# Reordering the work around the first token pair of a fused conditional-residual kernel: block chains ahead of combination splits, b1s cleared at another place, three copies on another engine

## The reference, cut to what matters

```
x = x + W0[a]^T x                                  # mixes the 64 tokens of a sequence, W0[a] is 64x64
x = x + x W1 + (x A1[a]) B1[a]                     # rank 16
x = x + x W2^T + 0.5 (x A2[l]) B2^T                # rank 32
x = x + x W3^T + 2 sum_e gate_e(x) (x A3_e^T) B3_e # 8 experts of rank 16, the top 2 of the logits
                                                   # x Wr^T + 5 onehot(g), softmax over the 2
```

## Time and profile before

| | |
|---|---|
| median of 3 runs | 541.6 us (541.12 to 542.69) |
| the profiled execution | 540.56 us, of it 538.8 us from first to last instruction |
| granted TensorE clock, mean | 0.997 |
| TensorE busy | 526.5 us |
| VectorE, ScalarE, GpSimd busy | 300.3, 183.4, 163.3 us |
| first token pair on TensorE | from 250.2 to 297.9 us |

### The profile page before, as it was taken

The page is one execution under the profiler, slowest core; times in us unless marked ns, Lnnn a source line. Parts: engine busy times, 40 slices in busy tenths (PEclk is TensorE's granted clock), DMA queues, the critical chain, the costliest instruction groups (busy, mean ns, idle before and its releaser), DMA issues.

```text
span 538.8 us, 8930 instructions
## 1 busy us (share of the span) xinstructions
PE 526.5 (98%) x2764; PEld 459.4 (85%) x2764; DVE 300.3 (56%) x638; ACT 183.4 (34%) x339; POOL 163.3 (30%) x250
## 2 busy tenths in 40 slices
PE   8999999999999999999889999999999999999996
PEld 7999999998888888888667888888888888888885
DVE  3851323389723323379868674664747547466463
ACT  5641312135122323255153333233323333233322
POOL 2501000002111111128643335444354343542400
PEclk9999999999999999999899999999999999999999
DMA  8803020013440202040430422214223142132302
GB/s 280 301 29 132 2 78 16 1 54 123 142 151 3 79 0 79 1 157 6 141 94 22 129 82 89 86 77 126 83 70 94 74 132 88 56 95 78 126 21 78
DMA packets 23246, 46.79 MB, mean 87 GB/s; under 512 B 6820, under 2 KB 11044, under 8 KB 23092
## 3 DMA queue, kind: packets, MB, share of 16 engines
q1 hardware_dynamic: 23028, 45.85, 25.5%
q0 software_dynamic: 192, 0.59, 0.3%
HBM read 33.39 MB, written 13.04 MB: 86 GB/s over the span
## 4 chain that ended last, share of the span: by engine, by line
PE 88%; DVE 4%; POOL 2%; issue 2%; DMA 1%; SPq 1%; POOLq 1%; ACT 0%; DVEq 0%
PE bank L1590 25%; PE bank L1456 16%; PE bank L1524 12%; PE bank L1579 6%; PE bank L1498 5%; PE bank L1510 5%; PE bank L1638 4%; PE bank L1472 4%; PE bank L1646 4%; PE bank L1641 1%; PE bank L1640 1%; PE bank L1653 1%; DMA w2raw<-in_w_dram 1%; PE bank L1600 1%; DVE ml L1033 1%
## 5 line engine op out<-in xcount | busy, mean ns | idle before, releaser
L1590 PE MATMUL bank<-t_hi,em_hi 128*128 128x512 f32 x168 | 57.2, 403 | 0.0
L1033 DVE TENSOR_TENSOR em_lo<-bank,em_hi 128x384 fp32r<-128x384 f32 (+2 forms) x40 | 19.3, 492 | 63.5 <-ACT em_hi L745 52.4
L1033 DVE TENSOR_TENSOR w1t_lo<-raw,w1t_hi 128x1024 fp32r<-128x1024 f32 x18 | 24.5, 1361 | 23.7 <-ACT w1t_hi L777 17.1
L1590 PEld LDWEIGHTS bank<-t_hi,em_hi 128*128 128x128 f32 x168 | 31.1, 189 | 7.0
L1524 PE MATMUL bank<-te,em_hi 128*128 128x512 f32 x144 | 34.9, 395 | 0.0
L609 POOL CAST em_hi<-tba 128x256 fp32r x32 | 14.4, 479 | 66.9 <-PE bank L1579 63.2
L745 ACT ACTIVATE em_hi<-bank 128x384 fp32r<-128x384 f32 (+1 forms) x24 | 11.3, 498 | 64.3 <-PE bank L1456 57.1
L1524 PEld LDWEIGHTS bank<-te,em_hi 128*128 128x128 f32 x144 | 27.1, 188 | 6.5
L576 POOL DMA_DIRECT2D b2scr<-b2stage x3 | 1.8, 594 | 90.9 <-DVE b2stage L1033 90.9
L1033 DVE TENSOR_TENSOR em_hi<-tmp,em_hi 128x512 fp32r<-128x512 f32 x22 | 15.1, 687 | 20.0 <-ACT em_hi L884 10.9
L1590 PE MATMUL bank<-ml,em_hi 128*128 128x512 f32 x63 | 25.5, 405 | 0.0
(11 more groups left out here) (283 smaller groups left out, 1603.2 us busy)
## 6 DMA issues: line engine op xcount, KB each, us to landing
raw<-in_x_dram SPq DMA_DIRECT2D x16, 512.0 KB, 3.9
b1s<-b1scr SPq DMA_DIRECT2D x32, 217.5 KB, 2.8
raw<-in_b1w_dram SPq DMA_DIRECT2D x10, 512.0 KB, 3.3
out_dram<-ef SPq DMA_DIRECT2D x16, 256.0 KB, 2.0
out_dram<-ost SPq DMA_DIRECT2D x16, 256.0 KB, 2.4
w2raw<-in_w_dram SPq DMA_DIRECT2D x7, 512.0 KB, 7.7
graw<-in_w3a3wr_dram SPq DMA_DIRECT2D x4, 768.0 KB, 8.4
b1scr<-b1stage SPq DMA_DIRECT2D x12, 256.0 KB
```

The lines of the kernel that those rows point to most:

```text
L1033: V.tensor_tensor(dst, src, f32(hi), ALU.subtract).then_inc(signal, 1)
L1590: ins = nc.tensor.matmul(to[:, :], left[a][:, k0 + k, :], m_right(right, z, k), start=(name in OPENS and n == 0), stop=(n == 3 * KH - 1), ...
```

## The change

In the last row pair and the first token pair:

- GpSimd clears b1s ahead of both `diagonal` calls rather than behind them.
- Quarter b21 of the last row pair is copied out by ScalarE (`row_out`) and not by VectorE; TensorE waits for `s_ra` in place of `s_rd`.
- ScalarE makes the `hi` parts of t3, t1, t2 in separately placed fronts and backs, the first three ahead of `xn_hi(0)`, and the B3 copy sooner.
- ScalarE also copies the two odd output pieces of the first pair (new function `first_ost_odd`).
- VectorE does the block chain's steps sooner; the `lo` parts of t1, t2 and t4 come at the end of its list, around and behind the last mixing splits. `combination_lo` is gone.
- TensorE's small steps of block 0 move by 1 to 3 matmuls within the groups.

```diff
         SPLIT_HI = ... "b11f", "b12f", "b21f", "b11b", "b22f", "b12b", "b21b", "b22b",
-                       "t3f", "t3b", "t1f", "t1b", "t2f", "t2b", "t4f", "t4b"
+                       "t3f", "t1f", "t1b", "t2f", "t3b", "t2b", "t4f", "t4b"
# GpSimd
             take(0, choose(0))
+            pool.wait_ge(s_rw, PRODUCTS * NR)
+            for s in range(2):
+                nc.gpsimd.memset(f32(b1s[s][:, D + C3:]), 0.0).then_inc(s_b1z, 1)
             pool.wait_ge(s_s0l, 1)
             pool.wait_ge(s_bdz, 2)
             diagonal(0, 0, 0)
             diagonal(1, 1, 0)
-            pool.wait_ge(s_rw, PRODUCTS * NR)
-            for s in range(2):
-                nc.gpsimd.memset(f32(b1s[s][:, D + C3:]), 0.0).then_inc(s_b1z, 1)
             take(1, choose(1))
# ScalarE
+            def first_ost_odd(n):
+                act.wait_ge(s_y, n + 1)
+                nc.scalar.activation(ost[n], bank[YB + 1][:, :], ACT.Copy).then_inc(s_yd, 1)
...
                 split_hi("b12", BACK)
+                act.wait_ge(s_rw, PRODUCTS * NR)
+                row_out(LASTR, "b21", bank[BB])
+                act.wait_ge(s_ra, 2 * NR + 1)
+                split_hi("b21", BACK)
                 act.wait_ge(s_radd, 3 * NR)
-                act.wait_ge(s_rd, NR)
-                split_hi("b21", BACK)
                 split_hi("b22", BACK)
...
+                combination_hi("t3", FRONT)
+                combination_hi("t1", FRONT)
+                combination_hi("t1", BACK)
                 xn_hi(0, YB)
+                combination_hi("t2", FRONT)
                 h1_t(0, 0)
-                combination_hi("t3")
+                act.wait_ge(s_b3, 16)
+                nc.scalar.activation(B3[0][:, :], b3raw[:, :], ACT.Copy).then_inc(s_b3h, 1)
+                combination_hi("t3", BACK)
                 h2_t(0, 0)
-                combination_hi("t1")
                 left_hi(1)
                 exp_of(0)
+                combination_hi("t2", BACK)
                 xn_hi(1, YB)
-                combination_hi("t2")
                 act.wait_ge(s_nar, 2)
                 act.wait_ge(s_pw, 3)
                 xm_hi(0, bank[BA])
+                h1_t(1, 1)
                 xm_hi(1, bank[BB])
-                h1_t(1, 1)
-                act.wait_ge(s_b3, 16)
-                nc.scalar.activation(B3[0][:, :], b3raw[:, :], ACT.Copy).then_inc(s_b3h, 1)
                 ght_hi(0, 0)
                 h2_t(1, 1)
-                combination_hi("t4")
+                combination_hi("t4", FRONT)
+                combination_hi("t4", BACK)
                 exp_of(1)
                 xn_hi(2, YB + 1)
-                ght_hi(1, 1)
...
                 xm_hi(0, bank[BD_])
                 ost_even(0, 0)
+                ght_hi(1, 1)
                 act.wait_ge(s_mix, 2)
                 xm_hi(1, bank[BC])
+                first_ost_odd(1)
                 ost_even(0, 2)
+                first_ost_odd(3)
# VectorE
-                dve.wait_ge(s_rw, made + PRODUCT["p4"])
-                V.tensor_copy(m_row(j, "b21"), bank[BB][:, :]).then_inc(s_rd, 1)
+                if j < LASTR:
+                    dve.wait_ge(s_rw, made + PRODUCT["p4"])
+                    V.tensor_copy(m_row(j, "b21"), bank[BB][:, :]).then_inc(s_rd, 1)
...
                 front_sum("t4")
+                second_low_rank(0, 0, steps)
                 dve.wait_ge(s_tb, FORMED["t1"])
+                dve.wait_ge(s_ml, SPLIT_LO["b12b"])
                 back_sum("t3")
-                second_low_rank(0, 0, steps)
-                combination_lo("t3")
+                split_lo("t3", FRONT)
+                split_lo("t3", BACK)
+                route(0, 0, steps)
                 dve.wait_ge(s_tb, FORMED["t3"])
                 back_sum("t2")
-                route(0, 0, steps)
                 dve.wait_ge(s_tb, FORMED["t2"])
                 back_sum("t4")
-                combination_lo("t1", "t2")
-                left_lo(1)
                 xn_lo(1, YB)
-                gates(0, 0, steps)
-                first_low_rank(1, 1, steps)
-                second_low_rank(1, 1, steps)
-                combination_lo("t2", "t4")
-                xm_lo(0, bank[BA], 1)
-                xm_lo(1, bank[BB], 2)
                 dve.wait_ge(s_b3h, 1)
                 lo(B3[1][:, :], b3raw[:, :], B3[0][:, :], s_b3l)
+                first_low_rank(1, 1, steps)
+                gates(0, 0, steps)
+                second_low_rank(1, 1, steps)
+                left_lo(1)
+                xm_lo(0, bank[BA], 1)
                 ght_lo(0, 0)
+                xm_lo(1, bank[BB], 2)
                 route(1, 1, steps)
                 gates(1, 1, steps)
                 xn_lo(2, YB + 1)
+                xm_lo(0, bank[BD_], 3)
+                dve.wait_ge(s_tf, FORMED["t2"])
+                split_lo("t1", FRONT)
                 ght_lo(1, 1)
-                xm_lo(0, bank[BD_], 3)
                 xm_lo(1, bank[BC], 4)
-                ost_odd(0, 1)
-                combination_lo("t4")
-                ost_odd(0, 3)
+                dve.wait_ge(s_tb, FORMED["t2"])
+                split_lo("t1", BACK)
+                dve.wait_ge(s_tf, FORMED["t4"])
+                split_lo("t2", FRONT)
+                dve.wait_ge(s_tb, FORMED["t4"])
+                split_lo("t2", BACK)
+                split_lo("t4", FRONT)
+                split_lo("t4", BACK)
# TensorE
-                pe.wait_ge(s_rd, NR)
+                pe.wait_ge(s_ra, 2 * NR + 1)
...
-                group(a12, "b21", 0, 0, 6, False)
+                group(a12, "b21", 0, 0, 9, False)
                 mixed(0, 0)
-                group(a12, "b21", 0, 6, 9, False)
...
+                group(a12, "b22", 1, 0, 3, False)
                 h1_across(0, 0)
-                group(a12, "b22", 1, 0, 5, False)
+                group(a12, "b22", 1, 3, 8, False)
                 h1_into(0, 0, 0)
-                group(a12, "b22", 1, 5, 9, False)
+                group(a12, "b22", 1, 8, 9, False)
...
-                group(a21, "b11", 2, 0, 6, True)
+                group(a21, "b11", 2, 0, 5, True)
                 h2_across(0, 0)
-                group(a21, "b11", 2, 6, 12, True)
+                group(a21, "b11", 2, 5, 12, True)
```

More of the change, by code:

```diff
@@ L358, in cond_resid_kernel @@
         SPLIT_HI = {n: i + 1 for i, n in enumerate(("b11f", "b12f", "b21f", "b11b", "b22f", "b12b", "b21b", "b22b",
-                                                    "t3f", "t3b", "t1f", "t1b", "t2f", "t2b", "t4f", "t4b"))}
+                                                    "t3f", "t1f", "t1b", "t2f", "t3b", "t2b", "t4f", "t4b"))}
         SPLIT_LO = {n: i + 1 for i, n in enumerate(("b11f", "b12f", "b21f", "b11b", "b22f", "b12b", "b21b", "b22b",
@@ L757, in split_hi, with combination_hi @@
                     nc.scalar.activation(dst[:, KF, :], raw_back(name), ACT.Copy).then_inc(s_mh, 1)
[L759 to L763, removed]
+            def combination_hi(name, part):
+                act.wait_ge(s_tf if part == FRONT else s_tb, FORMED[name])
+                split_hi(name, part)
             def plain_hi(dst, src):
@@ L1155, in split_lo @@
                     lo(out_, raw_back(name), dst[:, KF, :], s_ml)
[L1157 to L1164, removed]
             def plain_lo(dst, src, hi, count):
@@ L1355, in first_pair_lo @@
                 split_lo("b12", BACK)
-                dve.wait_ge(s_ml, SPLIT_LO["b12b"])
+                dve.wait_ge(s_ml, SPLIT_LO["b11b"])
                 back_sum("t1")
```

## The result

The changed kernel takes 537.55 us (median of 6 runs, 536.77 to 537.97), the kernel before 541.11 in the same rounds (6 runs). The ratio is 0.994, interval 0.9922 to 0.9958: faster by 0.6%, 3.6 us where 7.0 were forecast, and 537.55 lies just above the range. Its profiled execution took 537.65 us, span 535.9, clock 1.000.

A forecast was written before the change was run, and what follows sets the result against it. TensorE, busy 526.5 of 538.8 us, was taken as the bound. Removing 7.7 us of stops and low clock, less 0.1 and 0.6 of new waits, gains 7.0 us: forecast 534.6 us, range 533.2 to 537.4.

The forecast's parts named there:

- the five stops: TensorE's five waits between 260 and 292 us, first token pair: 5.30 us idle, 6.15 us with 0.17 added for each.
- low clock: TensorE's clock falls after the longest stop, slowing 13 matmuls; removing that stop was to save 1.56 us.
- b1s cleared sooner: GpSimd's clearing 7 us sooner, near 251.3, so the longest stop, 1.93 us, goes, with 5 us of slack.
- rival D: ScalarE's wait for b3raw delays h2_into; the kernel gets slower if it lands from 271 on; chance 0.02.
- First stop: TensorE's 0.51 us wait for xn_lo goes as VectorE starts sooner; ScalarE's added work costs nothing.
- Third, fourth and fifth stops: Waits of 1.46, 1.21 and 1.04 us go as VectorE's block chain and gates come sooner; 0.1 us left for gates.
- The bill: Postponed low splits on VectorE at the stage's end delay pair 1's h1_across: a new TensorE wait of 0.6 us.
- the sign of being wrong: Prediction wrong if the new wait before pair 1's h1_across exceeds 1.5 us.
- A: VectorE's t1, t2, t4 run beside GpSimd is 2 us longer or more, delaying pair 1: 538.0 us; chance 0.15.
- C: The gates are too slow beside GpSimd at both places, 0.5 to 1 us each: 536 us; chance 0.06.
- B: Clearing b1s is not what held the DMA, or SyncE's block lands no sooner: 538 us; chance 0.04.
- The sum: Whole kernel: 7.7 us of stops and clock loss gone, less 0.1 and 0.6 of new waits, gain 7.0 us.

The follow-up runs named there:

- e1: The kernel before with only GpSimd's clearing of b1s moved ahead of both diagonals: 538.10 us, ratio 0.9956 to the kernel before.
- e3: The changed kernel with the low splits of t1, t2 and t4 reading bank BD_ as minuend, one SBUF input each: 536.45 us, ratio 0.9929 to the kernel before.
- e4: The changed kernel with GpSimd's diagonal of block 2 ahead of its take of block 3: 540.05 us, ratio 0.9989 to the kernel before.
- e5: The changed kernel with GpSimd's index loads for take of block 1 moved ahead of the clearing: 536.07 us, ratio 0.9919 to the kernel before.
- e8: The changed kernel with both e5's early index loads and e6's splits in VectorE's gaps: 534.72 us, ratio 0.9899 to the kernel before.
- e9: e8 with GpSimd's identity add of block 2 moved ahead of take of block 3: 534.58 us, ratio 0.9888 to the kernel before.
- e6: The changed kernel with front splits moved up into VectorE's gaps and ScalarE's B3 copy behind h2_t: 536.03 us, ratio 0.9919 to the kernel before.
- e7: e8 with GpSimd's diagonal of block 2 ahead of take of block 3, block 3's index loads before both: 536.34 us, ratio 0.9933 to the kernel before.
- e2: The changed kernel with the b1s clearing put back behind both diagonals: 542.09 us, ratio 1.0032 to the kernel before.

## Why the prediction was right or wrong, point by point

- *What bounds the kernel, the five stops and their worth:* right for the execution that was read. All five went or nearly so, and the low clock with the second. But the 1.56 us of low clock stood in the sum as if every execution paid it, and 30 of 46 later ones did not. In e1 the DMA stop alone was worth 3.1, where the two terms give 1.93 + 1.56 = 3.5 and the stop behind it grew from 1.29 to 1.63.
- *b1s cleared sooner:* the stop went, by less slack than said. I put the clearing at 251.3, b1s landing at 258.2, the diagonals done at 258.7 ("start 0.3 us later"). Measured 254.4 for the clearing and 260.2 for the diagonals, 0.7 of each being the later stage. The step that failed first is here: I took over GpSimd's old times while handing its neighbour more two-input work. From it follow the b3raw and x landings later than said (b3raw at 266.4 for 263.4; ScalarE waited 2.97 for it, rival D's place, and `h2_into` started 0.2 late) and, with the index loads, the 1.08 before the second `narrow`, which I never placed: I said what it needs of VectorE and ScalarE and left out the `take` that it needs of GpSimd.
- *First stop:* right that it goes. "This costs nothing" was said of ScalarE's added work, and `xn_hi` and `mixed` were indeed not late. The price that I did not ask for was GpSimd's, by e1's rows against those after.
- *Third, fourth and fifth stops:* right, with 0.37 + 0.17 for the gates where I had 0.1. The gates took 3.4 us where I had 2.9, slowed by GpSimd's reads.
- *The bill:* the place was right, the size 0.6 was wrong: 1.73 + 0.16 idle, 2.2 us with the 0.17 for each, beyond the 1.5 that I had named as the sign of being wrong. Two terms failed. VectorE's own run was too short in my sum: it started 0.4 us later against p1 than I said and took 8.8 us to the CS split (287.23 to 296.07) where I had 7.6 + 0.3. Its h1c came 5.2 us after p1, where TensorE wants it 2.9 after; this alone makes the whole wait. And GpSimd's bd_lo, which `mixed` wants half a matmul group ahead of it, I never placed. I read the 1.99 of its identity add only as a sign that durations vary. The same add alone, later in that trace, shows what it had paid:

```profile
293.01 0.46 POOL L587 TENSOR_TENSOR ef<-ef,ident 128x128 f32<-128x128 f32 x1
```

  e3 shows what the shut-out is worth of this: without the second input GpSimd's part falls from 10.2 us (285.42 to 295.6) to 5.1, VectorE's run to the CS split from 8.8 to 8.0 and the stage from 53.21 to 52.06, and a wait of 1.00 for VectorE is left. e4 shows the other half: with bd_lo in time the wait moves to h1c, 1.24.
- *Rivals:* what happened is nearest to A (2.4 us of wait in pair 1, 538.0 forecast, 537.55 measured), which had 0.15. Its mechanism, VectorE late at that place, was right, but its run was 1.2 us longer and started 0.4 late, where A has 2, and GpSimd's chain stood beside it, which A does not name. That its time fits so well is luck: it reckoned with 1.56 of low clock, which came in some executions only, and left out the second `narrow` and the gates, 1.8 us. C happened in small, D only as the 0.2 us of `h2_into`, B not.
- *The sum:* the step that decides is "0.1 + 0.6" of new waits, measured 4.0, of which 1.25 is the second `narrow`, 2.2 pair 1, 0.5 the gates. The second step that failed is the 1.56 of low clock inside the 7.7: against executions without it the most that could go was 6.1.

Not tried: a version in which VectorE's t4 splits stand behind pair 1's CS split and h1 chain, since pair 1 shares its loop with the pairs after it on that engine.

## What to carry to other kernels

When work is moved into an engine's idle time, ask who was using that idle time: on a kernel where VectorE and GpSimd both read SBUF, a gap of VectorE is GpSimd's turn, and part of the price of filling it stands in the other engine's rows. Place every producer of the step that you expect next, not only those that the change touches. Ask how many executions pay for what one profile shows before you book it in full. And split an edit before building on it: here one memset moved in front was most of the gain, and the rest paid only once GpSimd's index loads and VectorE's splits had been placed anew around it.

## What the runs showed of the hardware

The shut-out is large and works both ways. In these traces a 128x128 subtraction on GpSimd takes 0.46 us alone and 1.84 beside front splits of 1.8 to 2.0; a VectorE addition of 8 columns takes 0.17 alone and 1.21 beside GpSimd.

TensorE's clock does not fall behind every stop of the same length. In the two profiles of the changed kernel TensorE stood still for 1.73 and 1.72 us at the same place; the windows behind it read 1.00 in the first and 0.66 in the second. In the second, 17 matmul rows start in 5 us where 19 did with a wait inside, and the stage is 54.38 us for 53.21. First the execution shown above, then the repeated one:

```profile
295.00:300.00 5.00, 4.19 (x19) 3.23 (x20) 2.86 (x8) 1.15 (x3) 3.71 (x5) 1.00 0.50 155
```

```profile
295.00:300.00 5.00, 4.96 (x17) 3.84 (x18) 2.73 (x7) 1.79 (x4) 3.15 (x5) 0.66 0.46 151
```

The same happened in e5 (0.66 behind 1.74 us) and in e4 (0.72 behind 2.08). For all executions, the longest stop in the stage, as profiled, and the share with a mean clock of 0.997 or less are:

| | longest stop, us | executions |
|---|---|---|
| e8, e9 | 0.67, 0.37 | 0 of 11 |
| e3, e6, e1 | 1.22, 1.36, 1.63 | 0 of 14 |
| e7 | 1.43 | 1 of 6 |
| changed kernel, e5 | 1.73, 1.74 | 4 of 18 |
| before | 1.76 | 16 of 46 |
| e4 | 2.08 | 7 of 10 |
| e2 | 2.97 | 8 of 9 |

So here a stop of some 1.7 us costs its length, and in some executions 1.2 to 1.6 us more, and the longer stops of e4 and e2 had the low clock in most executions. The mean clock does not say where it fell (other waits, of up to 1.9 us, stand early in the program), and what decides it at one length these runs do not show.
